# First attention of a two-layer kernel: probabilities and values as fp16 halves, turned by DMA, and ACT's norms one slot later

## What is computed

```python
q = _ln(_fp8_linear_pertensor(ln_out, wq, wq_scale, q_in_scale).reshape(b, s, g, hpg, d), qln_w, qln_b)
k = _ln(_fp8_linear_pertensor(ln_out, wk, wk_scale, k_in_scale).reshape(b, s, g, d), kln_w, kln_b)
v = _fp8_linear_pertensor(ln_out, wv, wv_scale, v_in_scale).reshape(b, s, g, d)
core = _gqa(q, k, v)            # softmax(q k / sqrt(d)) v, 16 heads of 128, 8 groups
...                             # the same with qx, kx, vx, where kx and vx come from the context
catq = _div_clamp_fp8(jnp.concatenate([core, xout], axis=-1), proj_smooth)
return jnp.einsum('bsi,oi->bso', catq, wproj) * (proj_in_scale * proj_w_scale)
```

## Time and profile before

| | us |
|---|---|
| median of 3 runs | 3264.55 (3263.78 to 3267.24) |
| the profiled execution | 3265.82 |
| its span, first to last instruction | 3263.6 |
| first attention, about | 0 to 1115 of the span |
| PE busy | 2882.3 (88%) |
| DVE, ACT, POOL busy | 1810.2, 1693.0, 1744.4 |

### The profile page before, as it was taken

How to read it: one execution, slowest core, us unless ns; L and a number is a source line. 1 busy time by engine, 2 the same in 40 slices (tenths; PEclk the granted TensorE clock), 3 DMA queues, 4 the chain that set the end, 5 groups by cost and what they waited for, 6 DMA issues and landing times. The chain is left out here.

```text
span 3263.6 us, 57383 instructions
## 1 busy us (share of the span) xinstructions
PE 2882.3 (88%) x16324; PEld 1652.9 (51%) x16325; DVE 1810.2 (55%) x5172; ACT 1693.0 (52%) x4502; POOL 1744.4 (53%) x2429
## 2 busy tenths in 40 slices
PE   4699999999999699999999996799989999625996
PEld 2366666666666445555555542344444444423663
DVE  4366666666666464334444353688888888321331
ACT  5577778778777433332333242566666666311331
POOL 6467777777776344434554453655655565240222
PEclk8799999999999899999999998999999999657998
DMA  6601101111110255544554474455555555327444
GB/s 236 232 27 43 43 29 36 43 38 35 39 42 23 95 167 161 153 130 137 161 152 129 144 212 100 78 109 109 106 103 106 107 106 101 96 100 264 84 84 106
DMA packets 459854, 348.33 MB, mean 107 GB/s; under 512 B 295728, under 2 KB 366512, under 8 KB 459696
## 3 DMA queue, kind: packets, MB, share of 16 engines
q1 hardware_dynamic: 396896, 267.79, 29.4%
q0 software_dynamic: 16640, 38.05, 5.8%
q10 hardware_dynamic: 46224, 41.36, 4.3%
HBM read 194.88 MB, written 93.50 MB: 88 GB/s over the span
## 5 line engine op out<-in xcount | busy, mean ns | idle before, releaser
L751 ACT ACTIVATE a_nrm<-a_mm,a_sc_t 128x128 f32<-128x128 f32 x768 | 291.4, 476 | 123.5 <-POOL a_sc_t L904 123.4
L1647 POOL TENSOR_TENSOR e_st<-e_st,e_ws_tile 128x1024 f32<-128x1024 f32 x64 | 123.5, 1930 | 427.4 <-PE e_y L1403 416.8
L602 DVE BATCH_NORM_STATS2 a_st<-a_mm 128x6 f32<-128x128 f32 x768 | 170.7, 284 | 291.2 <-PE a_mm L439 208.7
L438 PE MATMUL a_mm<-a_w_hi,a_xq_hi 128*128 128x512 f16 x768 | 297.4, 387 | 23.2 <-POOL a_xq_lo L886 15.0
L439 PE MATMUL a_mm<-a_w_hi,a_xq_lo 128*128 128x512 f16 x768 | 297.2, 387 | 0.0
L1441 ACT ACTIVATE e_hh<-e_ha 128x512 f16<-128x512 f32 x128 | 76.3, 596 | 414.7 <-PE e_ha L1388 413.5
L1536 DVE SCALAR_TENSOR_TENSOR e_hl<-e_ha,e_hh 128x512 f16<-128x512 f32 x128 | 88.5, 691 | 352.2 <-ACT e_hh L1441 351.8
L1812 PE MATMUL a_mm<-l_wh,a_src_hi 128*128 128x512 f16 x512 | 200.4, 392 | 76.0 <-DVE a_vl L1894 41.8
L903 POOL TENSOR_TENSOR a_sc_t<-a_sc_t,a_mhalf 128x4 f32<-128x4 f32 x192 | 204.3, 1064 | 117.8 <-DVE a_sc_t L609 117.5
L1401 PE MATMUL e_y<-e_w2h,e_hh 128*128 128x512 f16 x640 | 242.6, 379 | 0.0
L1402 PE MATMUL e_y<-e_w2l,e_hh 128*128 128x512 f16 x640 | 242.6, 379 | 0.0
(11 more groups left out here) (350 smaller groups left out, 8220.7 us busy)
## 6 DMA issues: line engine op xcount, KB each, us to landing
e_st<-in_w SPq DMA_DIRECT2D x128, 512.0 KB, 4.2
disp<-a_empty SPq DMA_DIRECT2D x16, 781.5 KB, 4.1
e_st<-in_w1b SPq DMA_DIRECT2D x32, 352.0 KB, 3.1
e_xb<-disp ACTq DMA_DIRECT2D x41, 260.5 KB, 2.7
disp<-a_empty SPq DMA_DIRECT2D x4, 2605.0 KB, 21.1
e_xb<-disp SPq DMA_DIRECT2D x40, 260.5 KB, 4.3
a_cx<-in_ctxT SPq DMA_DIRECT2D x32, 256.0 KB, 3.2
a_stage<-in_wprojT SPq DMA_DIRECT2D x16, 512.0 KB, 4.9
```

The costliest lines, as they stand in the source:

```text
L438: pe.matmul(out, xq_hi[:, n, c, :], w_hi[:, t, c, :], start=(c == 0), stop=False)
L751: ins = act.activation(nrm[:, n % 2, i * P:(i + 1) * P], src[:, i * P:(i + 1) * P], ACT.Identity, bias=sc_t[:, n % 2, 3, i:i + 1], scale=s ...
```

## The change

Values and probabilities are kept as two fp16 tiles each, a high half and the rest. ACT's `v_keep` writes the high half of the values, DVE's new `v_low` the low one (and now sets `v_ok`). ACT's new `p_high` takes the place of `p_keep`: it copies the probabilities, times 1024, to fp16; DVE's new `p_low` makes the rest; SP's new `p_turn` turns both by DMA, one transposing DMA each, and PE's `p_transpose` is gone. `pv` is three fp16 products in place of one fp32 product. `pv` and all that follows it stand one slot later, and so does ACT's `normalise` (offset 1 before, 2 after), while `q_transpose` and `q_keep` keep their offset of 3.

```diff
+            def p_turn(b, a):
+                for half, done in ((0, "p_hi"), (1, "p_lo")):
+                    sp.wait_ge(sem[done], at(a, NA, b))
+                    if half == 0 and not (isinstance(b, int) and b == 0 and a < 2):
+                        sp.sem_inc(sem["turning"], 1)
+                        sp.wait_ge(sem["pv"], at(a - 2, NA, b))
+                    sp.sem_inc(sem["turning"], 1)
+                    sp.dma_start_transpose(pT[half][:, a % 2, :].rearrange("p (i t) -> p i t", t=P),
+                                           pq[half][:, a % 2, :]).then_inc(turned[half][a % 2], 16)
-            run_pipeline(sp, [("job", 0, lambda b, t: weights(b, t + 1)), ("att", 5, residual), ("end", 10, store), ("in", 1, x_load)],
+            run_pipeline(sp, [("job", 0, lambda b, t: weights(b, t + 1)), ("att", 4, p_turn), ("att", 5, residual),
+                              ("end", 11, store), ("in", 1, x_load)],
...
             def pv(b, a):
                 vn = V_JOBS.index(JOBS.index(V_NAMES[KV_OF[a]]))
                 pe.wait_ge(sem["v_ok"], at(vn, NV, b))
-                pe.wait_ge(sem["p_ok"], at(a, NA, b))
+                for half in range(2):
+                    pe.wait_ge(turned[half][a % 2], 16 * at(a // 2, NA // 2, b))
...
-                    mm = pe.matmul(OVB[:, i * 256:(i + 1) * 256], vt[:, KV_OF[a], g * P:(g + 1) * P],
-                                   pT[:, a % 2, i * 256:(i + 1) * 256], start=True, stop=True)
+                    pe.matmul(OVB[:, two], vh, ph, start=True, stop=False)
+                    pe.matmul(OVB[:, two], vh, pl, start=False, stop=False)
+                    mm = pe.matmul(OVB[:, two], vl, ph, start=False, stop=True)
...
             run_pipeline(pe, [("job", 3, q_transpose), ("job", 0, project), ("att", 0, scores),
-                              ("att", 3, p_transpose), ("att", 5, pv), ("att", 9, out_project), ("in", 6, x_transpose),
-                              ("end", 14, r_transpose), ("end", 16, r_logits), ("end", 20, r_prefix)],
+                              ("att", 6, pv), ("att", 10, out_project), ("in", 6, x_transpose),
+                              ("end", 15, r_transpose), ("end", 17, r_logits), ("end", 21, r_prefix)],
...
+            def v_low(b, t):
...
+                    dve.wait_ge(sem["v_hi"], at(v_no[t], NV, b))
+                    dve.scalar_tensor_tensor(out=vt[1][:, i, :], in0=MMB[BANK[t]][:], scalar=scal[:, col:col + 1],
+                                             in1=vt[0][:, i, :], op0=ALU.mult, op1=ALU.subtract).then_inc(sem["v_ok"], 1)
+            def p_low(b, a):
+                dve.wait_ge(sem["p_hi"], at(a, NA, b))
+                if not (isinstance(b, int) and b == 0 and a < 2):
+                    dve.wait_ge(turned[1][a % 2], 16 * at(a // 2 - 1, NA // 2, b))
+                dve.scalar_tensor_tensor(out=pq[1][:, a % 2, :], in0=pr[:, a % 2, :], scalar=PS, in1=pq[0][:, a % 2, :],
+                                         op0=ALU.mult, op1=ALU.subtract).then_inc(sem["p_lo"], 1)
...
-            run_pipeline(dve, [("att", 2, row_scale), ("att", 1, smax), ("att", 6, o_quant), ("end", 10, final), ("end", 10, r_stats),
+            run_pipeline(dve, [("att", 2, row_scale), ("att", 1, smax), ("att", 4, p_low), ("att", 7, o_quant),
+                               ("end", 11, final), ("end", 11, r_stats),
...
+                               *(("in", at_, x_quant_of(n)) for n, at_ in enumerate(X_QUANT_AT)), ("job", 0, stats), ("job", 1, v_low),
...
-            def p_keep(b, a):
-                act.wait_ge(sem["ptr"], at(a, NA, b))
+            def p_high(b, a):
+                act.wait_ge(sem["pnorm"], at(a, NA, b))
...
-                               ("in", 9, convert_at(-1)), ("job", 3, q_keep), ("att", 1, exps), ("job", 1, normalise), ("job", 0, convert),
-                               ("att", 3, p_keep), ("job", 1, v_keep), ("in", 4, x_norm), ("in", 6, x_back),
+                               ("in", 9, convert_at(-1)), ("job", 3, q_keep), ("att", 1, exps), ("job", 2, normalise), ("job", 0, convert),
+                               ("att", 3, p_high), ("job", 1, v_keep), ("in", 4, x_norm), ("in", 6, x_back),
```

More of the change, by code:

```diff
@@ L250, in layer0_attention @@
         kT = s.sb("kT", [P, 4, DM], F32)
-        vt = s.sb("vt", [P, 4, DM], F32)
+        vt = [s.sb(f"v{n}", [P, 4, DM], F16) for n in ("h", "l")]
         nb = s.sb("nb", [P, 2, 4], F32)
@@ L255, in layer0_attention @@
         pr = s.sb("pr", [P, 2, DM], F32)
-        pT = s.sb("pT", [P, 2, DM], F32)
+        pq = [s.sb(f"pq{n}", [P, 2, DM], F16) for n in ("h", "l")]
+        pT = [s.sb(f"p{n}", [P, 2, DM], F16) for n in ("h", "l")]
         oy = s.sb("oy", [P, 2, DM], BF16)
@@ L271, in layer0_attention @@
             "x_in", "c_in", "x_stat", "x_scal", "x_norm", "x_tr", "x_t", "y_act", "y_pool", "xq", "xq_ok", "cx_hi", "cx_lo",
-            "mm", "stat", "scal", "norm", "v_ok", "qtr", "q_ok",
-            "score", "max", "exp", "rinv", "pnorm", "ptr", "p_ok", "pv", "oy", "cq", "proj",
+            "mm", "stat", "scal", "norm", "v_hi", "v_ok", "qtr", "q_ok",
+            "score", "max", "exp", "rinv", "pnorm", "p_hi", "p_lo", "turning", "pv", "oy", "cq", "proj",
             "xres", "x1", "out", "filled", "disp_filled", "rconst", "r_stat", "r_scal", "r_norm", "r_tr", "r_t",
             "r_lgt", "r_lg", "r_max", "r_exp", "r_mask", "r_px", "r_pos", "r_slot")}
+        turned = [[s.sem(f"turned_{n}{i}") for i in range(2)] for n in ("h", "l")]
         staged = [s.sem(f"staged{i}") for i in range(NSTAGE + LENT)]
@@ L402, in x_transpose @@
                 pe.wait_ge(sem["x_norm"], b + 1)
[L403 to L406, removed]
+                if isinstance(b, int) and b == 0:
                     pe.wait_ge(sem["small"], 16 * N_SMALL)
+                if not (isinstance(b, int) and b < 3):
+                    pe.wait_ge(sem["r_lg"], b - 2)
                 for c in range(KT):
@@ L462, in scores @@
                 mm.then_inc(sem["score"], 1)
[L464 to L480, removed]
             def pv(b, a):
@@ L505, in out_project @@
                 mm.then_inc(sem["proj"], 1)
-            def kept(a, b):
-                return min(at(a, NA, b), NA * B) if isinstance(b, int) else at(a, NA, b)
             def r_transpose(b, k):
-                pe.wait_ge(sem["p_ok"], kept(4, b + 1))
-                if isinstance(b, int) and b == B - 1:
+                if not (isinstance(b, int) and b == 0):
                     pe.wait_ge(sem["r_pos"], b)
@@ L528, in r_prefix @@
             def r_prefix(b, k):
[L529 removed]
+                pe.wait_ge(sem["x_t"], min(b + 4, B) if isinstance(b, int) else b + 4)
                 pe.wait_ge(sem["r_mask"], b + 1)
```

31 lines of the change are left out of this document (17 added, 14 removed).

## The result

The changed kernel takes **3592.62 us** (median of 4 runs, 3589.39 to 3596.26) against 3265.25 before (4 runs): a ratio of 1.1006, 95% interval 1.0993 to 1.102. The forecast was slower, 3497, within 3405 to 3565: the direction held, the size did not, 327 us more instead of 232.

What follows compares the result with a forecast made beforehand. PE was taken as the packed bound before, ACT's late normalise after. 10.9 us of waits plus 3.7 for the clock gave 14.6 per batch; 3265.8 + 215 + 15 + 3 − 1.3 = 3497 us, range 3405 to 3565.

Steps and rivals of the forecast that it cites:

- The ring: First attention, odd slots: PE's turn, ACT's copy, exponentials, normalise, back to PE, no spare slot; 4.25 us against PE's 2.16.
- a store every 75 to 80 us: Sign in the profile after: SP's interval between stores, one per batch, which was 63.45 us before.
- The pairs: Even slot plus next, normalise queued behind exponentials needing the maximum: 4+5 and 12+13 8.5 us each, 8+9 7.8, 0+1 10.3.
- The clock: Projections slowed behind PE's idle gaps: 0.75 × 1.7 us for two long gaps, a third for three others; 3.7 us per batch.
- Batch 0: Turning DMAs queue behind the fills, so three or four slots run after them: 15 us, between 0 and 30.
- The end: 14.7 full batches at 14.6 us each, and a drain with one more slot and a DMA for a turn, 3 us.
- The rival of a clock that falls at nearly every gap: Ring plus a clock term of 8 us per batch: some 3560 us; chance 0.15.
- PE's saving: PE's turns of probabilities go, fp32 products become fp16: 5.1 us less per batch, PE's work 63.0 to 57.9.
- the halves' price: DVE's low halves, 8.3 us, stay under PE's work; turning DMAs hidden: no cost, except 0.15 in 8+9 and 0.7 in 0+1.
- the faster rival: PE stays packed, the ring taking at most 2.16 us in odd slots: about 3192 us; chance 0.10.
- the forecast of 58.4: Batch time if PE stays packed: 63.45 − 5.1 us, the faster rival's batch.

Runs made afterwards that it cites:

- e4: Changed kernel with matmuls nobody reads added where PE would stand idle, from batch 1 on: 3511.9 us, ratio 1.0761.
- e1: Changed kernel with ACT's normalise back at offset 1, fp16 halves, turning DMAs and other offsets kept: 3338.2 us, ratio 1.0224.
- e3: Changed kernel with ACT's exponentials behind the same slot's normalise instead of ahead, normalise still at offset 2: 3341.3 us, ratio 1.0234.
- e12: e3 with p_high ahead of normalise, residual sum behind statistics and POOL's low part of the value input first in slot 0: 3481.0 us, ratio 1.0658.
- e17: e1 with p_high ahead of normalise, and products, rounding, output projection and what follows at the offsets of the kernel before: 3283.4 us, ratio 1.0061.
- e8: e1 without low halves: one turning DMA, three products on high halves only, PE's work the same: 3278.7 us, ratio 1.0045.
- e10: e1 with VectorE's residual sum behind the statistics and ACT's p_high ahead of normalise: 3314.9 us, ratio 1.0161.
- e14: Kernel before with values and turned probabilities kept as bf16, nothing else changed or moved: 3232.4 us, ratio 0.9904.
- e9: e1 with the residual sum behind the statistics and POOL's low part of the value input earlier in slot 0: 3330.2 us, ratio 1.0204.
- e11: e1 with residual sum and p_low behind statistics, p_high ahead of normalise, POOL's low part of the value input first: 3332.4 us, ratio 1.0209.
- e13: e10 with POOL's parts of the next batch's input set closer, so the value input is done one slot earlier: 3312.6 us, ratio 1.0152.
- e15: e13 with VectorE's rounding of the products (o_quant) behind its slot's statistics: 3388.0 us, ratio 1.0382.
- e16: Kernel before with values and turned probabilities kept as one fp16 tile each, nothing moved: 3232.8 us, ratio 0.9908.

## Why the prediction was right in kind and wrong in size

**The ring held.** At full clock (e4) the slots that it sets alone or with PE come out as worked out: 3 and 11 at 4.34 and 4.26 (4.25), 15 at 6.0 (6.0), 2, 10 and 14 at 4.57, 4.62 and 5.49 (4.58, 4.58, 5.44), 6 at 5.93 (5.87). e1, e3 and e12 show each in its way that it is a ring, and that its length is what ACT has between copy and norm. Of what was named to show the steps, PE's busy share (0.77 for 0.75), its waits and their releaser, and a clock under 1.00 came; a store every 75 to 80 us did not.

**The pairs were too short: the step that failed.** From the batch of e4's timeline above, head to head: 4+5 9.88 us (8.5 forecast), 12+13 9.45 (8.5), 8+9 9.36 (7.8), 0+1 11.12 (10.3), slot 7 4.59 (4.25): 5.0 us more a batch, and 0.2 in all other slots. The sum had added up single instructions as they ran in the kernel before. The changed kernel's own trace has nearly the same pairs, 4+5 9.90 and 12+13 9.45. There, in slots 12 and 13, the statistics started 2.9 us after the projection did, as expected, but one of their instructions took 1.09 us, where its group's mean before is 303 ns, and the maximum stood behind it. VectorE, then POOL:

```profile
717.42 0.89 DVE L594 BATCH_NORM_STATS2 a_st<-a_mm 128x6 f32<-128x128 f32 x4 [0.88 <-PE a_mm L445]
...
718.76 1.09 DVE L600 TENSOR_SCALAR a_sc_t<-a_mv,a_eps_s 128x4 f32<-128x4 f32 x1
...
719.84 0.68 DVE L621 TENSOR_REDUCE a_nb<-a_scb 128x4 f32<-128x512 f32 x1
```

```profile
718.79 1.04 POOL L879 TENSOR_TENSOR a_xqs<-a_y,a_isc 128x512 f32<-128x512 f16 x1
```

It ends with POOL's instruction of 718.79. In slot 5 the exponentials stood behind the next input's norm (ACT's rows of 765.93 and 766.65 above), which had waited for POOL, a stage that the sum did not have.

In 8+9 low values, the router's pick and low probabilities stood ahead of the statistics. I had put 0.15 us on the low halves there; e4 and after have 1.6 more for the pair. The 0.8 of 0+1 and the 0.3 of slot 7 are not traced to an instruction. The range had room for the pairs' sum being 1.5 us a batch too high, and none of its own for its being too low.

**The clock was too cheap:** 5.7 us a batch, forecast 3.7 (its terms, 2 × 1.28 and 3 × 0.43, add up to 3.8). The two make 21.8 instead of 14.6 a batch, and 14.7 × 7.2 = 106 us of the sum's error; the sum is 95 us short. **Batch 0** cost about the 15 us that were put on it. Before, PE goes on in slot 5 of batch 1 at 158.18, behind its projection; after, it is through that projection at 171.6, 13.4 us later. PE's long stand is about as long as before (20.54 us, 19.96 before), but it comes three slots earlier, in slot 2, and ends with a turning DMA, so the slots between run behind it, as forecast:

```profile
156.66 0.37 PE L487 MATMUL a_ovb<-a_ph,a_vh 128*128 128x256 f16 x1 [20.54 <-DMA a_pl<-a_pql]
```

**The end was counted too high:** the last two intervals between stores grow by 17.4 and 3.9 us (62.61 to 80.02, 30.33 to 34.24), not by 21.8 each, so 14.7 full batches and 3 us for the drain were too many, by some 10 us. That the total was not further off is luck: this error stood against the others. The rival of a clock that falls at nearly every gap was nearer (3560), but its clock term, 8 us a batch, was too high and stood in for the pairs. (PE's busy time does grow by that much, to 66.0 us a batch where 57.9 was worked out, yet e4 gets only 5.7 back.)

**PE's saving and the halves' price** were in the forecast as 5.1 us gained and nothing lost. The ring covered this, so it did not move the time; no run came near the faster rival's price (3192): the best one with both halves, e17, takes 3283. Without the ring the change costs 4.9 us a batch (e1) where −5.1 was worked out: 3.9 for low halves (e8) and 3.1 for the offsets (e10 to e17) make 7.0 of these 10, and 3 us are bubbles at the turn of the batch that PE's work covered before (e14). These are differences from different starting points and need not add up; no run leaves out the low halves at the old offsets. Of e1's 10 us, PE's windows give 3.1 to matmuls at a lower clock and the rest to idle time, so the clock, which the forecast of 58.4 left out, is part of both prices. That the bubbles come from the crowded queues of VectorE, ACT and POOL there is argued from their waits; e9, e11, e13 and e15 moved or added to them without removing them, and which link sets the 61.5 us of e14 stays open.

e14 and e16 are the versions that beat both kernels, 0.99 of before, with values and probabilities of one 16-bit tile each, which are coarser numbers than those of either kernel.

## What to carry to other kernels

Before moving a stage by a slot, follow the loop it closes: if the consumer's copy stands ahead of the next producer on one engine, the loop has to fit in one slot, and whatever stands between the two is its length. Where engines run a fixed order, a busy share of 99% says that one engine is full, not that the rest has room: lighten that engine alone, without the real change (e14 is one type), and see how much arrives before paying for the saving elsewhere.

## What the runs showed of the hardware

One VectorE instruction on 128x4 elements (the statistics' `tensor_scalar`) took 1.09 us beside POOL's work. Its mean over 350 to 950 us differs with the order of the stages, between runs whose engines are about as busy: 303 ns before, 353 after, 592 in e10, 319 in e17, with VectorE and POOL busy 463.16 and 453.79 of 600 us in e17 and 476.34 and 435.74 in e10. A few long ones make the mean: in e3 the median is 230 ns and the longest 2773. Rows of before, e10 and e17:

```profile
L608 DVE TENSOR_SCALAR a_sc_t<-a_mv,a_eps_s 128x4 f32<-128x4 f32 x113 | 34.2, 303 | 4.0
```

```profile
L600 DVE TENSOR_SCALAR a_sc_t<-a_mv,a_eps_s 128x4 f32<-128x4 f32 x107 | 63.3, 592 | 3.8
```

```profile
L600 DVE TENSOR_SCALAR a_sc_t<-a_mv,a_eps_s 128x4 f32<-128x4 f32 x112 | 35.7, 319 | 4.0
```

With 12 of them a batch, e10 to e17 is 3.3 us of VectorE's time, next to the 3.1 us that the offsets cost; whether the one causes the other was not tested. The Trainium skill (SBUF — State Buffer, Who interferes with whom) states that some single-source VectorE instructions share a port with POOL as an exclusive lock, the later one blocking. The end at POOL's end agrees; no run here isolates it, and the next instruction, of the same kind and shape, keeps a median of 162 ns in e3, its longest 180. And adding matmuls to idle time lowered the time by 81 us (e4), since those behind it then ran at 2.4 GHz.
